# Moving a norm and a self-attention from the back chain to the front chain of a pipelined transformer kernel

## The reference

```
x += xattn16(ln(x), ctx)            # layer 0: 16 heads, strided keys
x += distance_attn(ln(x))           # scores from pairwise distances, causal
x += moe(ln(x))                     # 8 experts, top 2, and a shared expert
y  = ln(x)                          # layer 1:  "y0"
y  = ln1(y + softmax(causal(y y^T / 16)) y)      # "y1"
y  = ln2(y + softmax(y ctx^T / 16) ctx)          # "y2"
x += ln3(y + ffn(y))
x += diff_attn_block(ln(x))         # differential attention and an ffn
x += product_key_memory(ln(x))      # top-16 keys of 64 x 64, 50 used rows
```

## Time and profile before

| | us |
|---|---|
| time, median of 3 runs (lowest to highest) | 3512.15 (3507.14 to 3529.97) |
| the profiled execution's own time | 3509.67 |
| its span in the trace | 3507.8 |

### The profile page before, as it was taken

The page is one execution under the profiler, slowest core; times in us unless marked ns, Lnnn a source line. Parts: engine busy times, 40 slices in busy tenths (PEclk is TensorE's granted clock), DMA queues, the critical chain, the costliest instruction groups (busy, mean ns, idle before and its releaser), DMA issues. The chain is left out here.

```text
span 3507.8 us, 47305 instructions
## 1 busy us (share of the span) xinstructions
PE 2613.3 (75%) x16384; PEld 1863.9 (53%) x16384; DVE 1927.4 (55%) x7470; ACT 937.8 (27%) x2008; POOL 667.4 (19%) x572
## 2 busy tenths in 40 slices
PE   5786898478884898758986689847898489876543
PEld 3574576255762567535664457625585256742421
DVE  3314564844847447664558556475384644674458
ACT  1212342123321233222421234212332124212210
POOL 0101132112312114021140112211130211402040
PEclk9897999689996999978998799968999699985766
DMA  6274163231523236040441416322261324503100
GB/s 227 73 258 154 41 207 105 98 115 65 200 84 107 85 103 225 26 156 31 153 175 37 152 57 202 113 105 88 78 213 62 116 72 135 193 29 110 25 0 6
DMA packets 211639, 392.64 MB, mean 112 GB/s; under 512 B 83344, under 2 KB 163472, under 8 KB 186160
## 3 DMA queue, kind: packets, MB, share of 16 engines
q1 hardware_dynamic: 205232, 372.49, 30.7%
q0 software_dynamic: 6144, 16.79, 1.4%
HBM read 350.55 MB, written 38.67 MB: 111 GB/s over the span
## 5 line engine op out<-in xcount | busy, mean ns | idle before, releaser
L796 PE MATMUL ps<-xbT,stream 128*128 128x128 f32 x2560 | 342.8, 291 | 12.3 <-ACT xbT L1122 6.1
L796 PEld LDWEIGHTS ps<-xbT,stream 128*128 128x128 f32 x2560 | 327.7, 205 | 36.3 <-issue 15.0
L299 POOL TENSOR_TENSOR hTB<-pb,sbuf 128x2048 f32<-128x2048 f32 x32 | 151.9, 4757 | 427.0 <-DVE pb L1656 427.0
L607 PE MATMUL ps<-cmat,aTB 128*128 128x512 f32 x256 | 159.4, 781 | 60.6 <-DVE sbuf L1740 56.9
L599 PE MATMUL ps<-ident,xnB 128*128 128x128 f32 x256 | 56.8, 341 | 163.8 <-DVE xnB L1285 127.5
L510 POOL DMA_INDIRECT hTA<-y_slots,slot x64 | 62.9, 982 | 606.6 <-DMA y_slots<-yb 589.6
L470 POOL TENSOR_TENSOR rstdA<-veA,mhalf 128x4 f32<-128x4 f32 x24 | 24.4, 1017 | 789.5 <-DVE veA L1278 789.5
L1013 PE MATMUL ps<-ident,work 128*50 128x128 f32 x32 | 12.5, 392 | 216.4 <-DVE work L1795 216.4
L809 PE MATMUL ps<-stream,hTA 128*128 128x256 f32 x640 | 163.6, 402 | 0.6 <-ACT yb L1143 0.6
L796 PE MATMUL ps<-xbT,ctxA 128*128 128x128 f32 x1280 | 157.4, 276 | 2.0 <-DMA ctxA<-in_experts 1.9
L796 PEld LDWEIGHTS ps<-xbT,ctxA 128*128 128x128 f32 x1280 | 151.4, 192 | 11.1 <-DMA ctxA<-in_experts 5.0
(11 more groups left out here) (277 smaller groups left out, 6001.0 us busy)
## 6 DMA issues: line engine op xcount, KB each, us to landing
stream<-in_experts SPq DMA_DIRECT2D x88, 1024.0 KB, 5.2
stream<-in_experts SPq DMA_DIRECT2D x88, 512.0 KB, 6.0
ctxA<-in_experts SPq DMA_DIRECT2D x40, 1024.0 KB, 5.1
work<-in_ctxT SPq DMA_DIRECT2D x32, 1028.0 KB, 6.9
hTB<-in_ctxN SPq DMA_DIRECT2D x32, 1024.0 KB, 6.9
down<-in_experts SPq DMA_DIRECT2D x40, 512.0 KB, 6.0
ctxA<-in_ctxT SPq DMA_DIRECT2D x16, 1024.0 KB, 8.8
stream<-in_ctxT SPq DMA_DIRECT2D x16, 1024.0 KB, 11.0
```

Of the source, the lines that this page charges most:

```text
L299: return e.tensor_tensor(out.rearrange("p (a d h) -> p a d h", a=8, d=16), a.unsqueeze(2).broadcast_to([P, 8, 16, 16]), vals[:, t, :].rear ...
L607: ins = mm(out, aT[:, k, t * P:(t + 1) * P], wt[:, k, cols], start=k == 0, stop=k == KT - 1)
L796: ins = mm(ps[:, 2 * (b % 2) + u, f * P:(f + 1) * P], wu[:, u, k, f * P:(f + 1) * P], xbT[:, b % 2, k, :], start=k == 0, stop=k == KT - 1)
```

## The change

1. The norm y0 and the causal self-attention with the addition of its result and the statistics of y1 move from the head of the back chain to the end of the front chain, behind `acc`. They use the front's tiles and PSUM banks 0 to 2 in place of 5 to 7.
2. y, not only x, must therefore cross to the next group: the group ends with a wait for POOL's gain additions and three copies (L1806 to L1808).
3. The tokens x are asked for first in SP's queue, by four DMAs of 128 KB with a semaphore each; the norm n0 takes its statistics tile by tile.
4. The final output goes to another tile, `xo`, since xnB now holds y, and two waits go (x4's for the gain additions, the y1 aggregation's for statistics).
5. `ORDER` is new, 198 steps as before.

The diff, without the edits of ACT, of names and semaphores, the removal of POOL's back part and the wait that x4 loses:

```diff
@@ -90,9 +90,10 @@
 
 
 ORDER = (
-    "bbbbbfbfbfbbbfbbfbbfbffbfbfffbfbfbfbfbbbfbbfbfbffbffbfbffbbbfbfbfbbfbbfbfbbbbbffbfbffbbfbfbfbfbb"
-    "fbfbbffbbfbfbfbfbbfbfbfbbfbbfbffbbfbbbbfbbbbbbbbbbbbbbbbfbbffbbbbbbfbbbfbbbbfbbbbfbbbbbfbbbbbfbb"
-    "bbbfbb")
+    "ffbfbfbfbfbffbfbffbfbfbfbfbfbfbbfbbfbfbfbffbffbbbfbbfbfbbfbfbffbbbbfbfbfbffbbbbffbbfbfbbfbbfbffb"
+    "bbfbfffbbbfbbfbfbbfbfbfbbbbbfbfbbbbbbbbbbbbbbbfbbfbbbbbfbffbfbfbbbfbfbbfbbbbbfbfbfbbffbfbfbfbfbb"
+    "bbbfbb"
+)
 
 
 def order(streams):
...
@@ -327,6 +332,9 @@
                 @block.sync
                 def _(sp):
                     rows = bass.ds(g * P, P)
+                    if "f" in streams:
+                        for t in range(T):
+                            sp.dma_start(xA[:, t, :], dram["x"][rows, t * D:(t + 1) * D]).then_inc(x_in[t], 16)
 
                     def front():
                         def late_weights():
...
@@ -336,8 +344,6 @@
                             sp.dma_start(wqp, dram["wqp"].rearrange("p (a d) -> p a d", a=NPH)).then_inc(late_in, 16)
                             sp.dma_start(keysp, dram["keysp"].rearrange("p (a k) -> p a k", a=NPH)).then_inc(late_in, 16)
 
-                        sp.dma_start(xA, dram["x"][rows, :].rearrange("p (t d) -> p t d", t=T)).then_inc(x_in, 16)
-
                         def context(t):
                             src = dram["ctxT"][rows, t * NCT:(t + 1) * NCT].rearrange("p (a n) -> p a n", n=NK)[:, :, 0:256]
                             sp.dma_start(ctxA[t % 2].rearrange("p k b n -> p (k b) n"), src).then_inc(ctxA_in[t % 2], 16)
...
@@ -420,7 +426,7 @@
                         rows_of(1)
                         sp.dma_start(ctxL[0:BT], dram["ctxL"][bass.ds((g - 1) * BT, BT), :].rearrange(
                             "p (t d) -> p t d", t=T)).then_inc(ctxl_in, 16)
-                        for _ in range(3 + T + 2 + 3):
+                        for _ in range(3):
                             yield
                         for i in range(T + 2):
                             if i < 2:
...
@@ -451,7 +457,7 @@
                                 yield
                             if i >= 1:
                                 sp.wait_ge(vec_done, V["x6", i - 1])
-                                sp.dma_start(dram["out"][grows, (i - 1) * D:i * D], xnB[:, i - 1, :]).then_inc(out_done, 16)
+                                sp.dma_start(dram["out"][grows, (i - 1) * D:i * D], xo[:, i - 1, :]).then_inc(out_done, 16)
                             for _ in range(3):
                                 yield
 
...
@@ -511,6 +517,14 @@
                                     yg[:, t, j, :], None, ys, bass.IndirectOffsetOnAxis(slot[:, t, j:j + 1], 0)).then_inc(got, 16)
                         yield
                         yield
+                        def last_gain(slot):
+                            if slot == 1:
+                                for t in range(T):
+                                    wait_scaled(pool, "y0", t)
+                                    add("xbe3", t, xA[:, t], xA[:, t], w["be3"])
+                        yield from norm("y0", veA, rstdA, last_gain)
+                        for _ in range(T + 2):
+                            yield
 
                     def back():
                         def with_bias(tag, be, dst):
...
@@ -840,10 +846,7 @@
                             yield
                         yield
                         yield
-
-                    def back():
-
-                        yield from norm("y0", xnB, (5, 6))
+                        yield from norm("y0", yA, (0, 1))
                         for i in range(T + 2):
                             if i < T:
                                 t = i
...
@@ -851,23 +854,24 @@
                                 if t >= 1:
                                     pe.wait_ge(vec_done, V["cs", t - 1])
                                 for k in range(KT):
-                                    ins = mm(ps[:, 5, 0:P], aTB[:, k, t * P:(t + 1) * P], aTB[:, k, t * P:(t + 1) * P],
+                                    ins = mm(ps[:, 0, 0:P], aTA[:, k, t * P:(t + 1) * P], aTA[:, k, t * P:(t + 1) * P],
                                              start=k == 0, stop=k == KT - 1)
                                 ins.then_inc(pe_done, PE.step("cs", t))
                             if 1 <= i <= T:
                                 t = i - 1
                                 pe.wait_ge(act_done, A["cexp", t])
                                 pe.wait_ge(act_done, A["cpT", t - 1] if t else A["y0", "T", 3])
-                                tr(ps[:, 6, 0:P], pb[:, t % 2, 0:P], ident).then_inc(pe_done, PE.step("cpT", t))
+                                tr(ps[:, 1, 0:P], pbA[:, t % 2, 0:P], ident).then_inc(pe_done, PE.step("cpT", t))
                             if i >= 2:
                                 t = i - 2
                                 pe.wait_ge(act_done, A["cpT", t])
                                 if t >= 1:
                                     pe.wait_ge(vec_done, V["y1p", t - 1])
-                                mm(ps[:, 7, 0:D], pT[:, t % 2, 0:P], xnB[:, t, :], start=True,
+                                mm(ps[:, 2, 0:D], pTA[:, t % 2, 0:P], yA[:, t, :], start=True,
                                    stop=True).then_inc(pe_done, PE.step("cpv", t))
                             yield
 
+                    def back():
 
                         yield from norm("y1", xnB, (5, 6))
                         for i in range(T + 2):
...
@@ -1265,14 +1269,15 @@
 
 
                         st, mv, ve, rstd, mr = small
-                        if before:
-                            before()
                         for t in range(0 if early else T):
+                            if before:
+                                before(t)
                             if t == 0 and V.n:
                                 own_steps()
                             vv.bn_stats(st[:, t, :], src[:, t, :]).then_inc(vec_done, V.step(tag, "st", t))
                         for t in range(T):
-                            v.wait_ge(vec_done, V[tag, "st", t])
+                            if tag != "y1":
+                                v.wait_ge(vec_done, V[tag, "st", t])
                             vv.bn_aggr(mv[:, t, :], st[:, t, :]).then_inc(vec_done, V.step())
                         own_steps()
                         vv.tensor_scalar(ve, mv[:, :, 1], EPS, None, ALU.add).then_inc(vec_done, V.step(tag, "var"))
...
@@ -1311,7 +1316,7 @@
 
                     def front():
 
-                        yield from norm("n0", xA, xnA, smallA, before=lambda: v.wait_ge(x_in, 16))
+                        yield from norm("n0", xA, xnA, smallA, before=lambda t: v.wait_ge(x_in[t], 16))
                         yield
                         hm = w["headmask"].unsqueeze(1)
                         heads_of = w["headmask"].rearrange("p (j h l) -> p j h l", j=4, h=2)[:, :, :, 0]
...
@@ -1539,31 +1544,29 @@
                                 vv.scalar_tensor_tensor(xA[:, t, :], yg[:, t, j, :], wpick[:, t, j:j + 1], xA[:, t, :], ALU.mult,
                                                         ALU.add).then_inc(vec_done, V.step("acc", t, j))
                         yield
-
-                    def back():
-
-                        yield from norm("y0", xB, xnB, smallB)
+                        yield from norm("y0", xA, yA, smallA)
                         for i in range(T + 2):
                             if i < T:
                                 t = i
                                 v.wait_ge(pe_done, PE["cs", t])
                                 if t >= 2:
                                     v.wait_ge(pe_done, PE["cpT", t - 2])
-                                vv.scalar_tensor_tensor(pb[:, t % 2, 0:P], ps[:, 5, 0:P], 1.0 / 16, w["causal"], ALU.mult,
+                                vv.scalar_tensor_tensor(pbA[:, t % 2, 0:P], ps[:, 0, 0:P], 1.0 / 16, w["causal"], ALU.mult,
                                                         ALU.add).then_inc(vec_done, V.step("cs", t))
                                 own_steps()
-                                vv.tensor_reduce(nm[:, t:t + 1], pb[:, t % 2, 0:P], AX.X, ALU.max, negate=True).then_inc(vec_done, V.step("cmax", t))
+                                vv.tensor_reduce(nmA[:, t:t + 1], pbA[:, t % 2, 0:P], AX.X, ALU.max, negate=True).then_inc(vec_done, V.step("cmax", t))
                             if i >= 2:
                                 t = i - 2
                                 v.wait_ge(act_done, A["cexp", t])
-                                vv.reciprocal(ri[:, 0, t:t + 1], rs[:, t:t + 1]).then_inc(vec_done, V.step())
+                                vv.reciprocal(riA[:, t:t + 1], rsA[:, t:t + 1]).then_inc(vec_done, V.step())
                                 own_steps()
                                 v.wait_ge(pe_done, PE["cpv", t])
```

(12 more changed lines are left out.)

40 lines of the change are left out of this document (18 added, 22 removed).

## The result

The changed kernel takes 3422.32 us (median of four, 3421.25 to 3433.42) against 3510.19 us: a ratio of 0.9745, with a 95% interval from 0.9704 to 0.9786. The forecast's sign and places were right, its sizes were not. A second measurement of both, in other runs, gave 3426.37 (ratio 0.9781, 0.9737 to 0.9825) for the changed kernel, and 1.0008 (0.9983 to 1.0033) for the kernel before against itself.

A forecast was written before the change was run, and what follows sets the result against it. PE waits in the head and VectorE limits the tail; iterations make 83% of the time. -13.4 + 9.8 - 2.9 = -6.5 us, seven times -45.5, gives 3467 us from a profiled 3509.67; range 3425 to 3520.

The forecast's parts named there:

- Head: From the residual's copy to the first k0: 18.5 us in place of 31.86, so -13.4 us an iteration.
- Tail: The last stretch, bound by DVE, takes in the moved chain's DVE work: +9.8 us an iteration, from 7.6 to 16.0.
- Middle: From k0 to the first top-k step: waits and half a block's work go, -2.9 us an iteration, from -5.8 to +3.0.
- the half block: Half a block's gate/up matmuls (x16, 2.02 us) move from the middle to the tail, beside DVE.
- so I keep half: In the middle's sum, -5.8 us is halved to -2.9, because a list laid out anew has new waits too.
- The two named waits: In the middle, 2.04 us before the second half of xs goes, and about 1.8 of 2.40 us at L731.
- Ends: Front-alone group gains the chain (+17.2, 0.8 for copies, less 0.5 for x), back-alone group loses 17.2: 0 in sum.
- D: Experts' rows come late for `acc` in the tail: DVE stands 20.9 us an iteration, 3613 us; chance 0.12.
- B: The moved chain isn't hidden in the last tile, so the tail costs 16.0 us: 3510 us; chance 0.10.
- X: In the head, the front's context shares the transfers with x's pieces: +3.8 us an iteration, 3494 us; chance 0.08.
- P: In the tail, DVE stands still while POOL does the gain additions: +2.9 us an iteration, 3487 us; chance 0.08.
- C: The new list gives more: middle -5.8 and tail +7.6 with head -13.4, -11.6 us, 3431 us; chance 0.13.

The follow-up runs named there:

- old_middle: The changed kernel with the old list of steps up to the last stage and the new one for the tail: 3490.53 us, ratio 0.9951.

## Why the prediction was right in sign and wrong in size

- **Head: -13.4 forecast, -12.6 measured** with the copies taken out. The parts in group 5: copy's end to SP's issue 2.19 us (1.49, and 0.8 for the added copies), issue to first transpose 7.79 (6.8 forecast: the issues take 2.67 us and not 1.4), transpose to k0 11.61 (10.2 forecast: q0 took 6.22 us, and the 4.70 of the front-alone group are inside the 7.4 of the sum). Right in its mechanism: x behind the context gave the head back, 31.8. That the size fits so well is in part luck: the parts came out 2.2 us too long, and the mean head of before, 33.9, is 1.3 longer than group 5's 32.6, from which they were taken off. In group 5 alone the head gained 10.3 us, copies included, where 12.5 were forecast.
- **Tail: +8.9 forecast, +7.0 measured.** DVE's busy time grew by 8.3, its idle time in the tail fell by 1.3. The 0.7 for hops and 0.5 for the last product were not there: DVE's idle time didn't grow, so the interleaving hides the hops. Left in a row at the end they cost 17.6.
- **Middle: -2.9 forecast, -9.4 measured** (-8.5 between the second profiles). This is the step that failed. The sum for the middle had two kinds of terms, waits that go and the half block that moves, and put PE's busy time for all other instructions at no change, without a reason. The middle's busy time fell by 6.5 us, from 261.4 to 254.9 (from 259.8 to 253.2 between the second profiles). The 18 records that moved are about 2 of them; the other 4.5 us are the same instructions at another granted clock, 31 us in seven iterations. The spread of the clock was on record in the trace that the prediction used: the seven middles of before took 294.2 to 308.6 us, at 0.97 to 0.91, for the same instructions. So group 5, the slowest of them, does not stand for all seven.
- **The step "so I keep half", in the same sum.** The two named waits went as priced: 2.04 us before the second half of xs to 0.00, 2.41 before L731 (now L737) to 0.69, as means of the seven. New waits did come, as that sentence feared: counted by the tiles that PE waits with, about 8.7 us an iteration grew or appeared (2.6 before the transposes of `pT`, 1.6 before those of `sbuf`) and 11.1 shrank or went. PE's idle time fell by 2.9 us (1.9 between the second profiles) of the 3.8 named. So half was near the truth for the waits; it was wrong for the half block's busy time, which moved whole (in `old_middle` other waits took part of it back). Together the halving gave away 1 to 2 us an iteration.
- **What that makes.** The middle was off by 6.5 us an iteration, 45 us in all, about as much as the whole forecast. That it equals the whole error is luck: head and tail, 1.1 us an iteration better than forecast, and the ends, 11 us worse, nearly cancel.
- **Ends: 0 forecast, +11 measured.** The last group gave 16.0 of 17.2 back. The first lost 27.0, of which 17.2 + 0.8 is the chain. The last down was 9.9 us later, with PE busy 7.7 us longer over the same 1290 records. The front-alone group with nothing moved took 283.0 us in the second profile of before, 284.6 with another list for the loop, and 285.5 and 294.0 in the two kernels with x asked for first and nothing moved; so most of the excess is in the profile that I started from and not in the change.
- **The rivals.** D was shown to be real by moving one matmul group: 13.2 us of waiting, 3516 us. In the change it has 6.6 us to spare. B fell, the chain is hidden in the last tile. X fell in the change: x's pieces land 3.0 us from issue to landing as the median, at most 4.0. Its price was wrong too: it took 11.11 us, issue to statistics, from 7.31 us, issue to first transpose. In group 0 x landed 3.7 us behind its issue, so the like difference is 7.4 us and not 3.8, and the run with x behind the back's context lost 9.6. P fell in the tail: GpSimd's four additions run from 1874.33 for 2.88 us beside the fourth tile's L1737 steps, which read PSUM and take 0.21 to 0.22 us as before, and the tail grew by less than the moved work. Rival P took the whole top-k to stand still. C, at 3431 with a chance of 0.13, was the nearest, and its two terms, a shorter middle and a smaller growth of the tail, went the right way.
- **The move, the list and x.** From the runs, of some 84 us: the list alone gave 34 (3506.5 to 3472.6), x first alone 40 (3509.4 to 3468.9), both together 55 (3507.9 to 3452.4), and the move on top of them 26 to 30. The parts do not add, since x and the list save some of the same waits.

## What to carry to other kernels

When two chains alternate in one list, ask of a list laid out anew not only which waits go but which waits stand right ahead of dense matmuls: at the place traced here a filled gap paid twice, by its length and by the rate of what follows. Take the mean of all iterations for the base, not one, and know how far two profiles of the same kernel lie apart before a term is made of the difference. And where a step moves from the end of a list to its inside, work out the slack of what it needs: here 6.6 us stood between a gain of 84 us and none.
